# A two-layer Mamba-2 kernel: dt in four passes, totals on VectorE, grouped output tile 0, and a new order of the scan step

## The reference

```python
for i in range(2):
    res = h
    h = _layernorm(h, ln_w[i], ln_b[i])
    zxbcdt = h @ in_w.T                      # 512 z, 512 x, 64 B, 64 C, 8 dt
    z, xBC, dt = jnp.split(zxbcdt, [512, 1152], axis=-1)
    dt = softplus(dt + dt_bias)              # one dt for each of 8 heads
    xBC = silu(causal_conv_4_taps(xBC) + conv_b)
    xh, Bm, Cm = split(xBC)                  # 8 heads of 64; state 64
    dA = exp(dt * -exp(A_log))
    # scan over tokens
    state = dA_t * state + (dt_t * x_t) B_t^T
    y_t = state C_t
    y = (y + D * xh) * silu(z)
    y = y * rsqrt(mean(y * y) + EPS) * rms_w
    h = y @ out_w.T + res
```

## Time and profile before

| | |
|---|---|
| time, median of 3 runs | 2013.32 us (2010.97 to 2015.57) |
| the profiled execution | 2011.51 us |
| its span, first to last instruction | 2009.7 us |
| PE busy | 1819.0 us (91% of the span) |
| DVE, ACT, POOL busy | 1565.4, 1258.7, 1195.9 us (78, 63, 60%) |
| TensorE's granted clock, mean | 0.975 of full speed |

### The profile page before, as it was taken

How to read it: one execution, slowest core, us unless ns; L and a number is a source line. 1 busy time by engine, 2 the same in 40 slices (tenths; PEclk the granted TensorE clock), 3 DMA queues, 4 the chain that set the end, 5 groups by cost and what they waited for, 6 DMA issues and landing times. The chain is left out here.

```text
span 2009.7 us, 36493 instructions
## 1 busy us (share of the span) xinstructions
PE 1819.0 (91%) x12544; PEld 1366.7 (68%) x12544; DVE 1565.4 (78%) x3311; ACT 1258.7 (63%) x2221; POOL 1195.9 (60%) x1032
## 2 busy tenths in 40 slices
PE   4899999999999999999999999999985698889898
PEld 3566676666676667766676776766764577777776
DVE  4677788887787776877777777777744799999986
ACT  3667666776666776667777676667740355555555
POOL 2466666666666654555555555555550586878785
PEclk9899999999999999999999999999996799999999
DMA  4011111111111111111111111111004201102001
GB/s 139 22 38 38 38 37 39 55 48 37 42 37 37 37 38 38 38 45 59 40 41 37 37 37 37 37 49 45 27 17 146 84 1 62 65 32 95 32 12 43
DMA packets 87271, 91.96 MB, mean 46 GB/s; under 512 B 4928, under 2 KB 82448, under 8 KB 87184
## 3 DMA queue, kind: packets, MB, share of 16 engines
q1 hardware_dynamic: 79360, 79.46, 12.2%
q10 hardware_dynamic: 7824, 11.37, 2.3%
HBM read 57.26 MB, written 25.17 MB: 41 GB/s over the span
## 5 line engine op out<-in xcount | busy, mean ns | idle before, releaser
L860 POOL TENSOR_TENSOR L_xc<-L_xpad,L_vec 128x512 f32<-128x512 f32 x160 | 166.1, 1038 | 318.1 <-ACT L_xpad L658 318.1
L852 POOL TENSOR_TENSOR L_yg<-L_yg,L_sz 128x512 f32<-128x512 f32 x128 | 165.4, 1292 | 159.5 <-DVE L_yg L1100 158.2
L382 PE MATMUL L_front<-L_uhi,L_whi 128*128 128x512 f32 x576 | 250.1, 434 | 9.5 <-DVE L_xc L1073 6.2
L1085 DVE TENSOR_TENSOR L_m<-L_dbank,L_gm 128x512 f32<-128x512 f32 x256 | 173.4, 688 | 101.8 <-ACT L_dbank L698 101.8
L530 PE MATMUL L_mix<-L_wo,L_yg 128*128 128x256 f32 x1024 | 235.4, 384 | 2.6 <-POOL L_yg L852 2.6
L382 PE MATMUL L_front<-L_uhi,L_wlo 128*128 128x512 f32 x576 | 229.2, 398 | 0.0
L382 PE MATMUL L_front<-L_ulo,L_whi 128*128 128x512 f32 x576 | 228.7, 397 | 0.0
L530 PEld LDWEIGHTS L_mix<-L_wo,L_yg 128*128 128x128 f32 x1024 | 191.9, 192 | 27.7 <-POOL L_yg L852 2.8
L658 ACT ACTIVATE L_xpad<-L_front,L_pbias 128x512 f32<-128x512 f32 x160 | 110.1, 688 | 153.1 <-PE L_front L382 153.1
L487 PE MATMUL L_ybank<-L_m,L_dtx 128*64 128x128 f32 x2048 | 158.1, 280 | 33.1 <-DVE L_yg L1100 25.6
L696 ACT ACTIVATE L_dbank<-L_dbank 128x512 f32<-128x512 f32 x256 | 148.7, 581 | 49.7 <-PE L_dbank L437 48.0
(11 more groups left out here) (176 smaller groups left out, 4949.3 us busy)
## 6 DMA issues: line engine op xcount, KB each, us to landing
h<-L_hres SPq DMA_DIRECT2D x32, 512.0 KB, 3.0
L_hin<-in_x SPq DMA_DIRECT2D x16, 512.0 KB, 4.7
L_hres<-in_x SPq DMA_DIRECT2D x16, 512.0 KB, 3.9
L_cc<-L_xc ACTq DMA_DIRECT2D x64, 128.0 KB, 2.3
L_hin<-h SPq DMA_DIRECT2D x16, 512.0 KB, 4.7
L_hres<-h SPq DMA_DIRECT2D x16, 512.0 KB, 3.8
M_hin<-h SPq DMA_DIRECT2D x16, 512.0 KB, 7.1
M_xin<-in_x SPq DMA_DIRECT2D x16, 512.0 KB, 7.1
```

Of the source, the lines that this page charges most:

```text
L382: last = nc.tensor.matmul(to[:, :], ww[:, kd, tile * P:(tile + 1) * P], a[:, kd, :], start=i == 0, stop=i == len(passes) - 1)
L852: nc.gpsimd.tensor_tensor(yg[:, t, :], yg[:, t, :], sz[:, t, :], ALU.mult).then_inc(y_gated, 1)
L860: nc.gpsimd.tensor_tensor(xc[p][:, q, :].rearrange("p (b i) -> p b i", b=NB), xpad[:, q, :, 0:P], vector(layer, "conv_w", q * TAPS, 1).uns ...
L1085: nc.vector.tensor_tensor(m[:, b, 4 * half:4 * half + 4, :], dbank[half][:, :].rearrange("p (h i) -> p h i", i=P), gm[:, b, :].unsqueeze(1 ...
```

## The change

It does five things in the scan step.

1. **dt in four passes.** `whi` gets eight more columns, the low part of dt's weights. A pass over `uhi` with 16 weight columns gives high and low products in rows 0 to 7 and 8 to 15; `ulo` meets the high columns alone. ACT keeps 16 rows, and DVE adds the two halves with the bias in two instructions (`dt_low`).
2. **Totals on VectorE.** `sum_da` leaves out the matrix of ones; DVE adds running sum and sum to the end (`total`).
3. **Output tile 0 grouped** as tiles 1 to 3 are, with one wait for all four `cs_done` ahead of it.
4. **The running sum is split in its PSUM bank.** `split_sums` reads it from `front[0]` and keeps the rests there; z tile 0 waits for `split`.
5. **A new order** of all four engines' lists.

```diff
-                passes = [(kd, a, ww) for kd in range(KD) for ww, a in ((whi, uhi), (whi, ulo), (wlo, uhi))]
-                for i, (kd, a, ww) in enumerate(passes):
-                    last = nc.tensor.matmul(front[0][0:NH, :], ww[:, kd, NPROJ - NH:NPROJ], a[:, kd, :],
+                passes = [(2 * NH, 0, uhi), (NH, 0, ulo), (NH, 1, ulo), (2 * NH, 1, uhi)]
+                for i, (wide, kd, a) in enumerate(passes):
+                    last = nc.tensor.matmul(front[0][0:wide, :], whi[:, kd, NPROJ - NH:NPROJ - NH + wide], a[:, kd, :],
...
-                for i, matrix in enumerate((tri, suffix, ones)):
+                for i, matrix in enumerate((tri, suffix)):
...
                 if t == 0:
                     pe.wait_ge(sums_out, n + 1)
+                    pe.wait_ge(split, 5 * n + 5)
...
                 if t == 0:
+                    pe.wait_ge(cs_done, NB * n + NB)
                     pe.wait_ge(m_done, 8 * n + 8)
...
-                if t == 0:
-                    for b in range(NB):
-                        pe.wait_ge(cs_done, NB * n + b + 1)
-                        within(n, t, b)
-                        last = carried(n, p, t, b)
...
-                nc.scalar.activation(dtT[0:NH, :], front[0][0:NH, :], ACT.Copy).then_inc(dt_kept, 1)
+                nc.scalar.activation(dtT[0:2 * NH, :], front[0][0:2 * NH, :], ACT.Copy).then_inc(dt_kept, 1)
...
+                nc.vector.tensor_tensor(dtlow[:, :, :], turned[:, :, NH:2 * NH], dtb[:, layer, :].unsqueeze(1).broadcast_to([P, NB, NH]),
+                                        ALU.add).then_inc(dt_low, 1)
+                dve.wait_ge(dt_low, n + 1)
+                nc.vector.tensor_tensor(dtraw[:, :, :], turned[:, :, 0:NH], dtlow[:, :, :], ALU.add).then_inc(dt_biased, 1)
...
-                cum = sums[:, 0, :, :]
+                cum = front[0][:, 0:NB * NH].rearrange("p (b h) -> p b h", b=NB)
+                rest1, rest2 = beside(0), beside(1)
+                part(0, cum)
                 dve.wait_ge(sums_out, n + 1)
-                part(0, cum)
+                nc.vector.tensor_tensor(total[:, :, :], cum, sums[:, 1, :, :], ALU.add).then_inc(total_done, 1)
```

More of the change, by code:

```diff
@@ L503, in outputs @@
                 wait(pe, y_skip, T * n + t - 1)
-                if t == 0:
-                    for b in range(NB):
-                        pe.wait_ge(cs_done, NB * n + b + 1)
-                        within(n, t, b)
-                        last = carried(n, p, t, b)
-                else:
-                    for b in range(NB):
-                        within(n, t, b)
-                    for b in range(NB):
-                        last = carried(n, p, t, b)
+                for b in range(NB):
+                    within(n, t, b)
+                for b in range(NB):
+                    last = carried(n, p, t, b)
                 last.then_inc(y_ready, 1)
@@ L560, in step @@
                 more, more2 = follows(n, 1), follows(n, 2)
-                decays(n, 4)
                 if more:
                     project_conv(n + 1, 0)
+                decays(n, 4)
+                turn_x(n, p, 0)
+                if more:
                     turn_dt(n + 1)
@@ L608, in step @@
                     decays(n + 1, 3)
-                square_sums(n)
-                if starts_layer(n + 2):
-                    fold_bias(layer_of(n, layer, 2))
                 if more2:
@@ L765, in step @@
                     raw_conv(n + 1, layer1, 1 - p, 3)
-                    softplus(n + 1)
-                    silu_conv(n + 1, layer1, 1 - p, 0)
-                    silu_conv(n + 1, layer1, 1 - p, 1)
-                square(n, 0)
-                if more:
-                    raw_conv(n + 1, layer1, 1 - p, 4)
-                    double_c(n + 1, 1 - p)
                 if more2:
@@ L775, in step @@
                 if more:
+                    softplus(n + 1)
+                    silu_conv(n + 1, layer1, 1 - p, 0)
+                    double_c(n + 1, 1 - p)
+                    raw_conv(n + 1, layer1, 1 - p, 4)
+                    keep_halo(n + 1, 1 - p)
+                square(n, 0)
+                if more:
+                    silu_conv(n + 1, layer1, 1 - p, 1)
                     silu_conv(n + 1, layer1, 1 - p, 2)
+                    silu_conv(n + 1, layer1, 1 - p, 3)
                 square(n, 1)
                 if more:
-                    keep_halo(n + 1, 1 - p)
-                    silu_conv(n + 1, layer1, 1 - p, 3)
-                    silu_conv(n + 1, layer1, 1 - p, 4)
                     silu_z(n + 1, layer1, 0)
@@ L904, in step @@
                 add_squares(n, 1)
+                add_squares(n, 2)
+                gate(n, 3)
+                add_squares(n, 3)
+                if more:
+                    second_operands(n + 1)
+                rsqrt(rrms, ssq, ss_done, n, rr_done)
                 if next_layer == 0:
                     norm_residual(n + 1, c + p, 1 - p)
-                gate(n, 3)
-                if more:
-                    second_operands(n + 1)
-                add_squares(n, 2)
-                add_squares(n, 3)
-                rsqrt(rrms, ssq, ss_done, n, rr_done)
             for g in range(GROUPS):
@@ L1221, in step @@
                     clear_halo(n, p)
+                mean_square(n)
                 if more:
@@ L1230, in step @@
                     rest_u(n + 2, 1)
-                mean_square(n)
+                finish(n, layer, c, p, 0)
                 if more:
                     weigh(n + 1, 2)
-                finish(n, layer, c, p, 0)
                 if starts_layer(n + 2):
```

127 lines of the change are left out of this document (67 added, 60 removed).

## The result

The change brings the kernel from 2013.98 to **1990.64 us** (median; 1986.75 to 1994.03 over 4 runs, beside 2010.97 to 2015.57): a ratio of 0.9885, with a 95% interval of 0.9862 to 0.9909. So it is 23 us faster, where 50 were forecast: the time lies inside the stated range (1920 to 1998), but not in the forecast's own band (1945 to 1980).

What follows compares the result with a forecast made beforehand. PE was taken as the bound. Per step, -1.60 work, -1.75 old waits, +0.6 and +1.3 new waits made -1.45 (first layer -1.77); over 16 and 15 steps 50 us, so 1963 us from 2013, range 1920 to 1998.

Steps and rivals of the forecast that it cites:

- The two old ones: PE's waits for `skip` 1 at output tile 3 (0.80 us) and for `finish` at `turn_x` 1 (0.81) would go.
- the chain to `turn_cum`: From conv tile 3 through ACT, POOL and DVE to conv tile 4's last tap, 13.5 us; PE waits 1.3 a step.
- the small ones: PE's waits of 0.1 to 0.25 us each at `turn_b`, `carry` 2, conv tile 3 and output tile 0, sum 0.6.
- the 0.3 at `turn_x` 1: First layer: two more `layer_moments` instructions ahead of `weigh` 3 delay DVE at `turn_x` 1 by some 0.3 us.
- The term -1.60: Work taken from PE per step: tile 0 grouping 0.94, dt 0.46 and the ones 0.20, together 1.60 us.
- Grouping: Output tile 0, grouped like tile 1, would take 2.00 us instead of 2.94, giving 0.94 a step.
- the other changes of mode in the step ... cancel: PE's tiling-mode changes outside tile 0, 20 before and 23 less 1 after, would add no net cost.
- The first and the last step go with them: The price of an ordinary step, taken 15 and 16 times, also covers the first and last step of the layers.
- A: Short wait at `turn_cum`, by shorter DMA hold or quicker split: 34 to 53 us more, 1929 to 1910; chance 0.22.
- B: The split's cast still collides, 0.8 us more at `turn_cum`, 1988, or small waits are larger; chance 0.17.
- C: `square_sums`, now ahead of `result` 0, makes PE wait for the square chain: 2036 to 2042 us; chance 0.08.
- D: The order costs elsewhere what it saves; only PE's work counts: -1.60 a step, 1964 us; no chance of its own.

Runs made afterwards that it cites:

- e2: The change with the two DMAs of `double_c` issued behind `raw_conv` 4 instead of ahead of it: 1955.80 us.
- e4: The change with output tile 0 alternating `within` and `carried` again, each block waiting for its own `cs_done`: 1992.20 us.
- e5: e2 with output tile 0 alternating `within` and `carried` again: 1972.44 us.
- e1: The change with `fold_bias` put back behind `result` 0 and `decays` 2 and 3 at the layer change: 1979.61 us.
- e9: e3 with `square_sums` behind `result` 0 again in the last item alone: 1942.72 us.
- e3: The change with both edits, `fold_bias` behind `result` 0 and `decays` 2 and 3, and the two DMAs behind `raw_conv` 4: 1947.68 us.
- e8: The change with the product with the matrix of ones made again in `sum_da` and not read: 1990.12 us.
- e11: The kernel before with four dt passes, totals on VectorE and the PSUM split, in the old order and without tile 0's grouping: 1989.42 us.
- e6: The change with the running sum split from its SBUF copy again, the rests in SBUF too: 1994.94 us.
- e10: The kernel before with four dt passes, totals on VectorE, the PSUM split and tile 0 grouped, in the old order on all engines: 2039.71 us.
- e12: e9 with PE's blocks joined again: `decays` 5 and 6 behind `turn_b`, `decays` 7 ahead of `carry` 2 and 3, `scores` moved: 1990.45 us.
- e7: The change with dt in six passes of eight weight columns again: 2004.19 us.

## Why the prediction was right in the waits and wrong in the size

- **The waits of the step: right.** The two old ones went; the chain to `turn_cum` was laid out as 13.5 us behind conv tile 3 and took 13.5; the wait was to be 1.3 and is 1.22. That the two lengths agree so well is in part luck: the split took 1.25 us for the 1.5 laid out, and the gaps ahead of the two DMAs and behind them, 0.17 and 0.16, were not laid out. Its cause, `double_c` ahead of `raw_conv` 4, is shown by e2: undoing it brings 35 us. All waits of a step in the second layer came to 1.64, against 1.85 by the forecast. In the first layer they fell by 0.86 instead of 0.17: the wait at `turn_cum` is nearer to 1.0 there (1.00 at 320.56), and the small ones and the 0.3 at `turn_x` 1 were taken too large.
- **PE's work: mis-sized, and this is the step that failed inside the layers.** The term -1.60 measured -0.86 in the second layer and -0.66 in the first. The ones were right (0.20, measured 0.21). dt was taken at 0.46 and is 0.32: the passes save 0.45, and the products around them take 0.12 more. Grouping was taken at 0.94, the difference of two neighbouring tiles in one trace; in the step it is 0.66 to 0.68 in the second layer and 0.37 to 0.45 in the first, in e4 and in e5. And the sentence that "the other changes of mode in the step ... cancel" failed: counting them (20 and 22) is no measure of what the order costs, and the order by itself adds 0.41 in the second layer and 0.38 in the first. That it is the changes of mode that cost this isn't shown: where it is known, it is `decays` and `scores` standing alone instead of joined. It is the largest error inside the step in the second layer; in the first, grouping is (0.37 for 0.94).
- **"The first and the last step go with them": wrong, and the costliest sentence.** It made three stretches that hold no ordinary step cheaper by 3.2 us together, without following `fold_bias`, `fold_weights` and the end through the new lists. They became dearer by 10.3. e1 shows the layer change's part and e9 the tail's, where the profile of the change is a mild one: e1 to e3, with the same code at the end, are 3.2 to 3.6 us above the kernel before between `turn_dt` of item 31 and the last `result`, the change 1.4. The 2.2 us of the first part are unexplained: conv tile 1 of the front already begins 0.8 later (30.17 for 29.34), and from run to run of nearly the same kernel the second `turn_dt` lies between 71.4 and 72.3 (before, 70.0).
- **The rivals.** A didn't come: `raw_conv` 4 was released by its own queue, as the forecast said. B's number came true (1988 for 1990.64) by another way: with its source in PSUM the cast doesn't collide, and the old waits did not return. C's mechanism is real and appears at the last two items alone (1.04 and 5.15 us), where its cover is missing: `turn_u` of a later item in both, the z tiles too in the last. D has the second layer's idle time right (it changed by 0.06) and fails with the work term.
- **A sum that the prediction took as plain.** A saving on the bound engine counts only up to the next wait behind it. e8 shows it at full loss (0.21 of work, nothing in the time), e4 almost, e11 in part.

## What to carry to other kernels

Split a forecast into the bound engine's work and its idle time for each stage, and follow edges (first item, layer change, last item) through the new order by themselves: one block that runs once cost here a quarter of what 29 steps brought. Before a queue gets a DMA issue ahead of a computation, ask who waits for that computation; swapping two lines was worth 35 us, more than the whole change. And grouping that needs all operands instead of the first pays only if the order first makes room for the last of them: the same edit brought 17 us in one order and cost 50 in another.

## What the runs showed of the hardware

- Two DMA issues on ACT's queue took 1.12 us (0.54 each in the median, 0.47 to 0.62 in the second layer), and the ACTIVATE behind them began 0.16 later: an issue holds what stands behind it like an instruction. It doesn't wait for the ACTIVATE ahead of it: in the kernel before the issues begin at 917.94, while `raw_conv` 4 runs from 917.73 to 918.42.
- A cast with source and result in SBUF that began beside a POOL instruction ended 0.04 to 0.06 us behind that instruction's end, whichever it was (`first_tap` before, `gate` in e6), and one with its source in PSUM took its 0.21 to 0.22 beside `gate`. What such a meeting costs is what is left of POOL's instruction.
- PE's granted clock fell during the 36 products of one column of `fold_bias`: 1.00 ahead of them, 0.75 during them, 0.65 in the 5.5 us behind. There `result` 0, the same 16 products that take 3.62 to 3.70 in the steps, took 5.63. The level 1.00 is 2.4 GHz, and 0.5 is 1.2 GHz; the products of one column kept PE busy in the records throughout, and yet the clock fell.

```profile
722.10:726.10 4.00, 3.29 (x27) 1.00 0.00 0
726.20:732.00 5.80, 5.80 (x40) 0.75 0.01 1
732.10:737.60 5.50, 5.50 (x17) 0.65 0.00 0
738.30:744.00 5.70, 0.00 (x0) 0.89 0.00 0
744.10:749.70 5.60, 5.59 (x15) 0.51 0.01 3
```

  Before, the same drop (0.74, then 0.62) fell on the short dt passes. Where `fold_bias` is put decides which products run slow.
- The clock also fell behind waits, in some steps and not in others. In e10, behind the 2.19 us of wait shown above, it was 0.68 from 322 to 326: `carried` of tile 0 took 1.97 us for 1.09 and `new_state` 1.77 for 1.08. Of 14 stretches of 44 us in the first layer, from 80 on, 9 had a mean of 0.96 and the others 1.00. In e12, behind the 1.10 us at `carry` 1, it was 0.59 from 885.8 to 890.0 and the conv passes began 0.42 apart instead of 0.23; 5 of 28 such stretches, over both layers, were below 0.99. The change, with one wait of 0.87 to 1.24 in each of its steps, was granted 1.00 in all but the first of these stretches (0.99), and the kernel before, with waits of up to 0.9, in all. So a single wait of that length doesn't decide it. That the pauses are the cause wasn't tried, and e7 had a stretch at 0.96 without more idle time than the change.
